# Attention and two hand-overs in a four-layer kernel: smaller pieces between TensorE and the engines that read it

## The reference, cut to what matters

```python
q = split_heads(x @ Wq + bq); k = split_heads(x @ Wk + bk); v = split_heads(x @ Wv + bv)   # 16 heads of 16
scores = jnp.einsum('bhqd,bhkd->bhqk', q, k) / jnp.sqrt(jnp.float32(dk))
scores = jnp.where(causal[None, None], scores, -jnp.inf)
attn = jax.nn.softmax(scores, axis=-1)
out = jnp.einsum('bhqk,bhkd->bhqd', attn, v)
```

## Time and profile before

| | |
|---|---|
| median of three runs | 1105.45 us (1102.81 to 1106.56) |
| the profiled execution's own time | 1107.4 us |
| its span, first to last instruction | 1105.7 us |
| mean granted TensorE clock | 0.985 of full speed |
| instructions | 21370 |
| ScalarE, POOL busy | 547.7 us, 394.3 us |

### The profile page before, as it was taken

How to read it: one execution, slowest core, us unless ns; L and a number is a source line. 1 busy time by engine, 2 the same in 40 slices (tenths; PEclk the granted TensorE clock), 3 DMA queues, 4 the chain that set the end, 5 groups by cost and what they waited for, 6 DMA issues and landing times.

```text
span 1105.7 us, 21370 instructions
## 1 busy us (share of the span) xinstructions
PE 1013.1 (92%) x7887; PEld 613.6 (55%) x7887; DVE 782.9 (71%) x1756; ACT 547.7 (50%) x1158; POOL 394.3 (36%) x605
## 2 busy tenths in 40 slices
PE   6999899999999998999999998989999998989766
PEld 3455546654555656754555666655455666657442
DVE  4888635678889755678889746678889636676526
ACT  4888621346888321446888311446888211431302
POOL 3566301132676011132666011132765101131652
PEclk9999999999999999999999999999999999999968
DMA  6899400003444000003444000004445704005657
GB/s 214 306 293 312 128 1 19 1 2 99 144 139 138 2 1 20 20 2 108 136 143 134 1 0 20 20 2 124 134 141 167 166 1 115 20 2 152 197 189 299
DMA packets 74743, 113.64 MB, mean 103 GB/s; under 512 B 6167, under 2 KB 64670, under 8 KB 73744
## 3 DMA queue, kind: packets, MB, share of 16 engines
q1 hardware_dynamic: 71952, 104.48, 30.5%
q0 software_dynamic: 1536, 3.60, 1.0%
q10 hardware_dynamic: 1152, 4.19, 0.9%
HBM read 93.46 MB, written 19.40 MB: 102 GB/s over the span
## 4 chain that ended last, share of the span: by engine, by line
PE 63%; DVE 14%; ACT 7%; issue 7%; POOL 5%; DMA 2%; SPq 0%; DVEq 0%; POOLq 0%; ACTq 0%
PE bank L970 25%; PE bank L1066 4%; PE bank L1157 3%; PE bank L1274 3%; PE bank L1320 3%; DVE hf L1876 3%; PE bank L1174 2%; PE bank L1364 2%; PE bank L1367 2%; PE bank L983 2%; DMA x<-cum_dram 2%; PE bank L961 2%; PE bank L1419 1%; PE bank L1081 1%; DVE hf L1890 1%
## 5 line engine op out<-in xcount | busy, mean ns | idle before, releaser
L970 PE MATMUL bank<-uT,w_in 128*128 128x512 f32 (+1 forms) x584 | 274.1, 608 | 6.8 <-DVE hf L1890 3.7
L1876 DVE SCALAR_TENSOR_TENSOR hf<-bank,conv_w,hf 128x510 f32<-128x510 f32 (+2 forms) x224 | 162.6, 743 | 34.6 <-ACT nmax L1550 20.0
L970 PEld LDWEIGHTS bank<-uT,w_in 128*128 128x128 f32 (+1 forms) x584 | 102.4, 188 | 126.8 <-issue 91.1
L1702 POOL TENSOR_TENSOR rs<-ve,half 128x2 f32<-128x2 f32 x56 | 38.9, 695 | 283.4 <-DVE ve L2028 283.3
L1533 ACT ACTIVATE hf<-bank,conv_b,conv_w 128x512 f32<-128x512 f32 x128 | 99.2, 775 | 53.8 <-PE bank L970 53.4
L970 PE MATMUL bank<-uT,w_gu 128*128 128x512 f32 x224 | 98.5, 593 | 0.0
L1157 PE MATMUL bank<-hf 64*64 64x128 f32 (+3 forms) x2048 | 88.1, 304 | 8.6 <-ACT x_pad L1577 3.5
L1157 PEld LDWEIGHTS bank<-hf 64*64 64x64 f32 x2048 | 74.0, 133 | 38.4 <-issue 30.7
L2325 DVE TENSOR_REDUCE nmax<-bank 128x2 f32<-128x256 f32 (+1 forms) x128 | 65.4, 553 | 20.4 <-PE bank L1367 18.2
L1511 ACT ACTIVATE xc<-bank 128x512 f32<-128x512 f32 x44 | 26.3, 597 | 104.1 <-PE bank L970 77.0
L970 PEld LDWEIGHTS bank<-uT,w_gu 128*128 128x128 f32 x224 | 42.4, 190 | 47.8 <-issue 47.3
(11 more groups left out here) (349 smaller groups left out, 2162.1 us busy)
## 6 DMA issues: line engine op xcount, KB each, us to landing
hf<-cum_dram SPq DMA_DIRECT2D x32, 384.0 KB, 3.5
dec<-cum_dram SPq DMA_DIRECT2D x32, 384.0 KB, 3.8
tmp<-cum_dram SPq DMA_DIRECT2D x32, 384.0 KB, 3.6
x<-cum_dram SPq DMA_DIRECT2D x32, 384.0 KB, 3.8
y_dram<-xf SPq DMA_DIRECT2D x16, 512.0 KB, 6.5
w_in<-in_w_in SPq DMA_DIRECT2D x1, 3584.0 KB, 11.4
w_in<-in_w_egu SPq DMA_DIRECT2D x6, 512.0 KB, 9.7
w_in<-y_dram ACTq DMA_DIRECT2D x5, 512.0 KB, 9.4
```

The source lines that it names most:

```text
L970: mm = pe.matmul(plan[key][0:n, :], w[:, k, cols], uT[:, k, :], start=k == 0, stop=k == DC - 1)
L1702: pool.tensor_tensor(rs[:, cols], ve[:, cols], half[:, cols], ALU.pow).then_inc(rstd_ready.sem, 1)
L1876: ins = dve.scalar_tensor_tensor(d, x, conv_w[:, j, TAPS - 1 - s:TAPS - s], d, ALU.mult, ALU.add)
```

## The change

It has these parts. (1) The transposes before the low-rank layer and the first half of those before the attention go into two banks, one for each chunk of 128 channels; ScalarE copies them one by one, and the products go by chunk, so that the first can use one chunk while the other is copied. `hw` is transposed and copied by tile. (2) The wait for the last two gated chunks moves to where the first tile uses them. (3) The mask comes from 32-row products: four for each head, 64 columns each, on the row block of the head; two bf16 constants replace the mask and the bf16 identity. (4) The second scores are planned by head: from pair 3 in three rotating banks (1, 4, 5), from pair 12 in four; ScalarE takes the exponential by head, POOL waits by head. (5) Products with V go into bank 0 (two exceptions), both parts in one step; VectorE's `outputs` moves one step ahead, and the turned maxima move to bank 0. (6) The transposes ("T", "moe", 1) move from bank 6 to bank 5.

```diff
+        def bank_of_turned(k, i):
+            u = 2 * k + i
+            if k < 3:
+                return 4 + i
+            return (1, 4, 5)[(u - 6) % 3] if k < 12 else (3, 1, 4, 5)[(u - 24) % 4]
...
-                plan.use(("T", "moe", 1), 6, r - 1)
+                plan.use(("T", "moe", 1), 5, r - 1)
...
-            plan.use(("T", "att", 0), 6, r)
+            for c in range(DC):
+                plan.use(("T", "att", 0, c), 4 + c, r)
...
-            for k in range(APAIRS):
-                plan.use(("ST", k), 2 if k > 11 and k % 2 == 0 else 4, r)
             plan.use(("NM", 0), 1, r)
...
+            for k in range(APAIRS):
+                for i in range(2):
+                    plan.use(("ST", k, i), bank_of_turned(k, i), r)
+            plan.use(("NM", 1), 0, r)
             for f in range(APAIRS // 2):
-                if f % 2 == 0 and f < 6:
-                    plan.use(("NM", f // 2 + 1), 1 if f < 4 else 6, r)
-                plan.use(("OT", f), f % 2, r)
+                plan.use(("OT", f), 2 if f == 5 else 1 if f == 7 else 0, r)
+                if f == 1:
+                    plan.use(("NM", 2), 0, r)
+            plan.use(("NM", 3), 6, r)
...
+        def transposes_by_chunks(pe, stage, n, src, j, r):
+            pe.wait_ge(u_ready.sem, u_ready.at(r, 2 * n - 1 + j))
+            for c in range(DC):
+                key = ("T", stage, j, c)
+                pe.wait_ge(*plan.before(key, r))
+                for i in range(2):
+                    mm = pe.transpose(plan.of(key, r)[:, i * P:(i + 1) * P],
+                                      src[:, 2 * j + i, c * P:(c + 1) * P], ident[:, :])
+                mm.then_inc(plan.fills(key, r), 1)
...
-                for f in range(FF // P - 2, FF // P):
-                    pe.wait_ge(*plan.drained(("U", f), r))
...
                         for f in range(FF // P):
+                            if t == 0 and f >= FF // P - 2:
+                                pe.wait_ge(*plan.drained(("U", f), r))
...
-                    transposes(pe, "lora", 2, u, j, r)
-                    pe.wait_ge(*plan.drained(("T", "lora", j), r))
-                    for t in (2 * j, 2 * j + 1):
-                        pe.wait_ge(*plan.before(("L", t), r))
-                        for k in range(DC):
+                    transposes_by_chunks(pe, "lora", 2, u, j, r)
+                    for k in range(DC):
+                        pe.wait_ge(*plan.drained(("T", "lora", j, k), r))
+                        for t in (2 * j, 2 * j + 1):
...
-                        for i in range(2):
-                            pe.matmul(on_diagonal(S[:, i, :]), ident_bf[:, :], qkey_mask[:, :], start=True,
-                                      stop=False, skip_group_check=True)
+                        for part in range(P // HKEYS):
+                            for i, (h, rows) in enumerate(heads):
+                                pe.matmul(of_key_part(S[:, i, :], part), mask_rows[rows, part, :],
+                                          mask_keys[rows, :].unsqueeze(1).broadcast_to([HKEYS, 2, HKEYS]),
+                                          start=part == 0, stop=False, skip_group_check=True)
...
-                        pe.wait_ge(*plan.before(("ST", k), r))
+                        if k == 12:
+                            pe.wait_ge(*plan.drained(("S", APAIRS - 1), r))
+                        for i in range(2):
+                            pe.wait_ge(*plan.before(("ST", k, i), r))
...
-                add_at = {9: (0, (0,)), 10: (0, (1,)), 11: (1, (0,)), 12: (1, (1,)), 13: (2, (0,)), 14: (2, (1,)),
-                          15: (3, (0,)), 16: (3, (1,)), 17: (4, (0, 1)), 18: (5, (0, 1)), 20: (6, (0, 1))}
+                add_at = {9: (0, (0, 1)), 11: (1, (0, 1)), 13: (2, (0, 1)), 15: (3, (0, 1)), 17: (4, (0, 1)),
+                          18: (5, (0, 1)), 20: (6, (0, 1))}
...
+            def turned_by_chunks(stage, j, r):
+                for c in range(DC):
+                    key = ("T", stage, j, c)
+                    act.wait_ge(*plan.full(key, r))
+                    act.activation(uT[:, c, j * HALF:(j + 1) * HALF], plan.of(key, r)[:, 0:HALF], ACT.Copy)\
+                        .then_inc(plan.drains(key, r), 1)
...
                 for k in range(APAIRS):
-                    act.wait_ge(*plan.full(("ST", k), r))
-                    if k >= 6:
-                        act.wait_ge(*plan.full(("OT", (k - 6) // 2), r))
-                    act.activation(prT[k % 6], pair_banks(("ST", k))[:, :, 0:TRI], ACT.Exp)\
-                        .then_inc(plan.drains(("ST", k)), 1)
+                    for i in range(2):
+                        act.wait_ge(*plan.full(("ST", k, i), r))
+                        if k >= 6 and i == 0:
+                            act.wait_ge(*plan.full(("OT", (k - 6) // 2), r))
+                        act.activation(prT[k % 6][:, i, :], plan.of(("ST", k, i), r)[:, 0:TRI], ACT.Exp)\
+                            .then_inc(plan.drains(("ST", k, i), r), 1)
...
-                    if n >= 10 and n % 2 == 0:
-                        outputs(n // 2 - 5)
+                    if n >= 9 and n % 2 == 1:
+                        outputs((n - 9) // 2)
...
-                outputs(3)
                 keep_maxima(3)
```

More of the change, by code:

```diff
@@ L33 @@
 KEYS = P // 2
+HKEYS = 32
 TRI = 3 * P
@@ L346, in sandwich @@
             for j in range(2):
-                plan.use(("T", "lora", j), 4 + j, r)
+                for c in range(DC):
+                    plan.use(("T", "lora", j, c), 4 + c, r)
             for t in range(TILES):
                 plan.use(("L", t), t, r)
-            for j in range(2):
-                plan.use(("LT", j), 4 + j, r)
+            for t in range(TILES):
+                plan.use(("LT", t), 4 + t % 2, r)
             if r == 0:
@@ L986, in first_linears, with of_key_part @@
                         mm.then_inc(plan.fills(key), 1)
-        def on_diagonal(bank):
-            return bank[:, :].rearrange("p (b n) -> p b n", n=P)[:, 0:3:2, :]
+        def of_key_part(bank, part):
+            both = bank[:, :].rearrange("p (b n) -> p b n", n=HKEYS)
+            return both[:, part:part + 2 * P // HKEYS + 1:2 * P // HKEYS, :]
         def x_block(t, q, hq):
@@ L1322, in queries_or_keys @@
                     mm.then_inc(plan.fills(key), 1)
[L1324 to L1328, removed]
+                transposes_by_chunks(pe, "att", 3, u, 0, r)
+                for k in range(DC):
+                    pe.wait_ge(*plan.drained(("T", "att", 0, k), r))
+                    for c in range(DC):
+                        for name in "QK":
+                            key = (name, c, 0)
+                            if k == 0:
+                                pe.wait_ge(*plan.before(key, r))
+                            mm = pe.matmul(plan.of(key, r)[:, 0:HALF],
+                                           w_att[:, k, "QK".index(name), c * P:(c + 1) * P],
+                                           uT[:, k, 0:HALF], start=k == 0, stop=k == DC - 1)
+                            if k == DC - 1:
+                                mm.then_inc(plan.fills(key, r), 1)
                 def values(j):
@@ L1640, in _ @@
                             shared_sum(0, r - 1)
-                    act.wait_ge(*plan.full(("LT", j), r))
-                    act.activation(hwT[:, j * HALF:(j + 1) * HALF], plan[("LT", j)][:, 0:HALF],
-                                   ACT.Copy).then_inc(plan.drains(("LT", j)), 1)
+                    for t in (2 * j, 2 * j + 1):
+                        act.wait_ge(*plan.full(("LT", t), r))
+                        act.activation(hwT[:, t * P:(t + 1) * P], plan[("LT", t)][:, 0:P],
+                                       ACT.Copy).then_inc(plan.drains(("LT", t)), 1)
                 def keep_queries_or_keys(name, c, j):
@@ L2425, in _layouts @@
     k, q = np.arange(128)[:, None], np.arange(128)[None, :]
-    low = np.where(q >= k, 0.0, -1e30).astype(f)
     att = [i["L1_attn_" + n] for n in ("Wq", "Wk", "Wv", "Wo")]
@@ L2449, in _layouts @@
                             + [(0.25, s) for s in (np.arange(128) % 32 < 16, np.arange(128) % 32 >= 16)]], 1).astype(f),
-        "qkey_mask": np.concatenate([low.T, low.T], 1),
+        "mask_rows": np.concatenate([(q < 32 * h + k % 32).astype(f) for h in range(4)], 1),
         "row_parts": rows.reshape(128, 3, 16),
-        "earlier": (k < q).astype(f),
+        "mask_keys_earlier": np.concatenate([np.where(np.arange(32)[None, :] == k % 32, -1e30, 0.0).astype(f),
+                                             (k < q).astype(f)], 1),
         "late_keys": np.where(q >= (k + 64) % 128, 0.0, 1e30).astype(f),
```

47 lines of the change are left out of this document (25 added, 22 removed).

## The result

The changed kernel takes 1098.13 us (median of 5 runs, 1094.80 to 1098.52) against 1104.97 us for the kernel before on the same chip: ratio 0.9936, 95% interval 0.9917 to 0.9955, so 5 to 9 us faster. The forecast was 1093.4 us, range 1087 to 1101. The profiled execution took 1098.52 us with a span of 1096.8 us (before: 1105.7).

A forecast was written before the change was run, and what follows sets the result against it. TensorE was taken to bound the kernel, busy 92% of the span, with VectorE next in part of the attention. The terms summed to 12.0 us won, taking the median to 1093.4 us, range 1087 to 1101.

The forecast's parts named there:

- Rival (b): Attention: VectorE paces it whatever the banks do, or waiting for both heads' banks keeps the loop closed; 1098.2 us, chance 0.18.
- down projection's wait: Before the down projection: moving the wait for gated chunks removes a 0.90 us stop a round; 3.6 us won.
- hand-over by chunk: Before expert choice and before queries and keys: copying transposed rows in halves saves 0.42 us each; 3.4 us won.
- mask: Attention scores: eight 32-row matmuls take 0.24 us instead of 0.31 in seven steps a round, plus two steps; 3.0 us won.
- second scores and products, turn to turn: Attention steps 9 to 16: banks by head remove the scores' wait for exponentials; 1.0 us a round, 4.0 us won.
- turn for quarter 1 behind the key copy: Attention: turned maxima move to bank 0, behind the last key copy, some 0.1 us later; 0.4 us lost.
- end of the stage (POOL): End of attention: POOL masks the last pair by head, so its power comes 0.2 us earlier a round; 0.8 us won.
- bank 5: Routed tokens' second-half transposes wait for VectorE's tap to release the bank; 0.73 us in three rounds, 2.2 us lost.
- constants: Kernel start: one constant 128 KB larger, another 16 KB, while TensorE's first work waits for them; 0.2 us lost.
- rival (c): The wait on bank 5 is caught up and VectorE's full idle is returned; 1089.2 us, chance 0.12.
- hwT by tile: Saves some 0.15 us of a copy, on a branch ready before VectorE asks; put at nothing.
- uT's 0.25 us: Sign of being right: the waits on uT before L1293 and L1320 stand at about 0.25 us.

The follow-up runs named there:

- e1: Changed kernel with second scores, exponentials, masking and products with V put back as before the change: 1093.51 us, ratio 0.9899 to the kernel before.
- e4: Changed kernel with the turned maxima of quarters 1 and 2 in bank 2 instead of bank 0: 1090.70 us, ratio 0.9876 to the kernel before.
- e8: Changed kernel with turned maxima in bank 2, second scores' bank waits moved later, and routed transposes in bank 6 again: 1087.04 us, ratio 0.9838.
- e10: Changed kernel with transposed rows handed over whole again before expert choice and queries and keys, hwT by halves: 1101.66 us, ratio 0.9974.
- e11: Changed kernel with turned maxima in bank 2 and routed transposes in bank 6 again, without later waits of second scores: 1087.50 us, ratio 0.9858.

## Why the prediction came out right, and where it was wrong

Six of the eight terms came within 0.6 us; the one for the attention's loop had the wrong sign, and the turn for quarter 1 cost three times its price. That the time still fell into the range is in part luck: the loss was smaller than the sum of the rest, of which three terms ran 0.4 to 0.6 us over. Rival (b)'s 1098.2 is almost the measured 1098.13 us, but that is chance too: its terms are not those of the table, and VectorE does not pace that stretch of the changed kernel. By the stages, four rounds (three for bank 5), without falls of the clock:

| Term | predicted | measured |
|---|---|---|
| down projection's wait | 3.6 | 4.2 |
| hand-over by chunk | 3.4 | 3.8 |
| mask | 3.0 | 3.5 |
| second scores and products, turn to turn | 4.0 | -1.4 |
| turn for quarter 1 behind the key copy | -0.4 | -1.3 |
| end of the stage (POOL) | 0.8 | 1.1 |
| bank 5 | -2.2 | -2.0 |
| constants | -0.2 | 0 |
| sum | 12.0 | 7.9 |

The mask's 3.5 us are 0.59 us a round ahead of the turn for quarter 0 and 0.29 us between the turns (25.24 us from quarter 0 to 3 before, 24.96 us in e1, which has the new mask and the old attention). The attention's terms are the changed kernel against e1: 16.75 against 16.41 us, 8.87 against 8.55 us, and 12.96 against 13.22 us at the end of the stage, where the power starts 1.44 us behind the start of the last exponential instead of 1.74 us. The two spans differ by 8.9 us, and by 8.2 us once the falls of the clock are taken out: 2.65 us in the changed kernel's attention, 1.7 us in the first round of the kernel before (6.97 us from the first queries to the first mask instead of 5.28 us) and about as much in its last round. The medians differ by 6.8 us, about 1 us less than 7.9.

Where it went wrong: "I take 1.0 us a round, 4.0 us (bounds 0 and 1.5 a round, the idle itself)". The step was built on the wait for exponentials and on VectorE's idle time. It did see the other two users of bank 0, "one wait on the single bank of the products" and the turn of maxima "behind the last key copy", and priced both. It did not put the third question to that bank: what stands behind the maxima in it. The products do, and they could no longer run under keep_maxima. With the maxima in bank 2 (e4) the same loop gains 1.12 us a round against e1, close to the 1.0 us predicted. So the size was about right, though scores still stop up to 0.6 us for exponentials in e4, and what was missed is the wait that the change adds in bank 0. A lower bound of 0 was wrong too: a change of banks adds waits as well as taking them away, so the loss had no reason to be excluded.

- The down projection's 4.2 us lie outside the bounds (2.8 to 4.0). The 0.90 us is TensorE's idle time, counted from the end of the record before; from start to start the way over the same eight records is 4.49 us before (406.75 to 411.24) and 3.44 us after (403.85 to 407.29).
- The turn for quarter 1 did stand behind the last key copy, as worked out, but 0.32 us a round later and not 0.1 us.
- The exponentials were sized well: 0.49 us by head, two in 0.87 us (estimated 0.49 and 0.88). But "with banks by head ... this wait goes" was wrong: a step without products waits 0.64 us for the first head's exponential, since three banks leave the next pair only one free. Rival (b) named this; it was given 0.18. Its other half, VectorE as the pace, is true only once bank 0 is free and the late waits are in (e8).
- Bank 5 went as worked out: a stop of some 1.6 us released by the tap, the projection 0.73 us later by the sum and 0.74 us by the rows (1.71 less 0.97), and next to nothing caught up behind it, so rival (c) falls.
- The constants cost nothing that can be told: the scan's first product starts at 35.60 us (34.76 before), but kernels with the same constants have it between 34.07 and 36.08 us.
- The mask went as worked out: 0.13 us from mask to scores and 0.09 us more ahead of the mask make 0.22 us (estimated 0.24), and the four steps n 5 to 8 gained 0.29 us (8.84 us before, 8.55 us in e1), 0.07 us each as forecast. What ran over, 0.1 us a round, lies ahead of the turn for quarter 0.
- hwT by tile, put at nothing, shortened the waits ahead of its products (L1328 in e10, L1332 in the changed kernel) from 4.6 to 3.2 us in all; what that alone is worth was not tried.
- Of the signs named ahead, "no score waiting for an exponential" and "VectorE nearly without idle" failed; the absent "issue", uT's 0.25 us, the stop released by VectorE's tap (1.2 to 1.6 us) and the mask records of two heads starting together came. Two signs of being wrong came as well: scores still released by exponentials, and keep_maxima(3) no earlier (17.2 us behind the turn for quarter 1, 16.9 us before).

## What to carry to other kernels

When a plan of banks changes, list for every bank who reads it next and who writes it after that, over the whole stage: a wait that was removed by rotating one group came back through a bank that two others share. Move the result that is read at once into a bank whose reader has just finished (here bank 2, whose scores the maxima had just taken), and let independent work stand behind a turn, not its dependants. A right total is no evidence for its terms: only undoing the parts one by one showed that one of them cost time.

## What was not expected of the hardware

Apart from the last 80 us, where every profile shows it, TensorE's granted clock fell to its lower level, 1.2 GHz, for some 3 to 7 us once or twice in seven of the thirteen profiles, at places that change from one execution of the same kernel to the next, and each fall cost 1.3 to 2.65 us: in the changed kernel's profile at 474 us, in its second at 238 us, in that of the kernel before at 200 us and at 995 us. The stretch before the first of these:

```profile
470.00:474.00 4.00, 2.42 (x50) 1.86 (x50) 3.36 (x10) 1.89 (x5) 2.17 (x6) 1.00 0.00 0
```

TensorE had been busy 2.42 of 4 us there; in the 2 us at whose end the fall in the second profile began, it had been busy 1.82 us (236 to 238 us). Of the eight profiles of kernels with the 1.06 us stops, five show a fall between step 9 and the turn for quarter 3 and one just behind it; of the four profiles without these stops (e1, e4, e8, e11) none does, and the kernel before, without them too, falls at other places. Thirteen profiles are few, and the stops' part in it is not settled.
